# Two kinds in one slot: 84 half tiles in 42 slots in place of 45 whole tiles

## The reference

```python
x = x + gnn(layernorm(x), src/dst edges, edge_type)
t = layernorm(x)
hs     = gelu(t @ sw1[n].T + sb1[n])         # 2 shared experts, hidden 64 each
shared = sum_n hs[n] @ sw2[n].T + sb2.sum(0)
probs  = softmax(t @ gate_w.T + gate_b)      # 8 routed experts
cw     = probs where among the top 2 of a row, else 0
hr     = gelu(t @ rw1[e].T + rb1[e])         # hidden 64 each
routed = sum_e cw[:, e] * (hr[e] @ rw2[e].T + rb2[e])
x = x + shared + routed
```

## Time and profile before

| | us |
|---|---|
| median of 3 runs (lowest, highest) | 1600.99 (1600.15, 1612.06) |
| the profiled execution's own time | 1598.47 |
| its span | 1596.7 |
| PE busy | 1491.6 (93%) |
| DVE, ACT, POOL busy | 927.9, 705.7, 662.6 |
| five bare slots, 1459.68 to 1514.16 | 54.48 |
| four slots with group work, 1247.66 to 1299.35 | 51.69 |

### The profile page before, as it was taken

One profiled execution on the slowest core, in us unless ns is written; L12 is line 12 of the kernel. 1 busy time (PEld: TensorE's weight loads), 2 busy tenths in 40 slices (PEclk: granted clock), 3 DMA queues, 4 the chain that ended last, 5 costly groups with the idle time before them and its releaser, 6 DMA issues. The chain is left out here.

```text
span 1596.7 us, 27768 instructions
## 1 busy us (share of the span) xinstructions
PE 1491.6 (93%) x8680; PEld 1200.0 (75%) x8680; DVE 927.9 (58%) x2667; ACT 705.7 (44%) x1231; POOL 662.6 (41%) x989
## 2 busy tenths in 40 slices
PE   6999998989898999999999986599999999999997
PEld 4777666777786677777888864478888888888986
DVE  5555686867752333334766556566666767665453
ACT  3334334556652212122666535446565656453322
POOL 3762232457753000000467634546546464543222
PEclk9999999999999999999999998699999999999999
DMA  9999999597757999999667688879776776534220
GB/s 243 277 279 286 298 294 304 190 289 131 128 91 170 295 290 279 278 292 272 157 126 133 106 214 175 236 204 249 224 233 191 221 213 200 167 129 131 93 75 3
DMA packets 130212, 325.95 MB, mean 204 GB/s; under 512 B 17115, under 2 KB 17641, under 8 KB 129698
## 3 DMA queue, kind: packets, MB, share of 16 engines
q1 hardware_dynamic: 84626, 211.19, 44.8%
q0 software_dynamic: 45456, 113.12, 31.1%
HBM read 205.62 MB, written 121.74 MB: 205 GB/s over the span
## 5 line engine op out<-in xcount | busy, mean ns | idle before, releaser
L1207 ACT ACTIVATE th<-bank 128x512 fp32r<-128x512 f32 x158 | 94.2, 597 | 291.7 <-PE bank L1487 291.6
L1005 POOL DMA_INDIRECT gx<-y,dst_slot x42 | 46.2, 1101 | 266.1 <-ACT xn_e L1227 243.0
L1842 DVE SCALAR_TENSOR_TENSOR tl<-bank,th 128x512 fp32r<-128x512 f32 x79 | 54.4, 689 | 162.3 <-ACT th L1207 162.0
L1139 POOL DMA_INDIRECT out<-xt,out_row x90 | 93.2, 1035 | 128.4 <-DVE xt L2198 92.3
L1467 PE MATMUL bank<-root2h,th 128*128 128x512 f32 x316 | 133.1, 421 | 12.6 <-DVE tl L1842 7.8
L1467 PE MATMUL bank<-root1h,th 128*128 128x512 f32 x316 | 131.6, 416 | 7.9 <-DVE yout L1869 4.8
L1869 DVE TENSOR_TENSOR yout<-bank,bias_b 128x512 f32<-128x512 f32 x150 | 102.3, 682 | 45.4 <-DMA y<-yout 18.7
L1467 PE MATMUL bank<-root2l,th 128*128 128x512 f32 x316 | 126.0, 399 | 0.0
L1467 PE MATMUL bank<-root2h,tl 128*128 128x512 f32 x316 | 125.2, 396 | 0.0
L1467 PE MATMUL bank<-root1l,th 128*128 128x512 f32 x316 | 125.0, 396 | 0.0
L1467 PE MATMUL bank<-root1h,tl 128*128 128x512 f32 x316 | 124.1, 393 | 0.0
(11 more groups left out here) (355 smaller groups left out, 4378.8 us busy)
## 6 DMA issues: line engine op xcount, KB each, us to landing
basis_t<-in_gnn_basis SPq DMA_DIRECT2D x64, 896.0 KB
xt<-sorted_rows SPq DMA_DIRECT2D x45, 560.0 KB, 3.9
xin<-in_x SPq DMA_DIRECT2D x39, 512.0 KB, 8.8
xin<-y SPq DMA_DIRECT2D x39, 512.0 KB, 8.5
y<-yout SPq DMA_DIRECT2D x37, 512.0 KB, 9.2
z<-yout SPq DMA_DIRECT2D x34, 512.0 KB, 8.4
stage1q<-in_x SPq DMA_DIRECT2D x5, 1024.0 KB, 7.5
stage2q<-in_x SPq DMA_DIRECT2D x5, 1024.0 KB, 8.7
```

The lines of the kernel that those rows point to most:

```text
L1005: pool.indirect_dma_start(out=gx[:, e % 6, :], out_offset=None, in_=x if pr.phase == SB else y1, in_offset=bass.IndirectOffsetOnAxis(ap=ds ...
L1139: pool.indirect_dma_start(out=out, in_=xt[i % 4][:, j, 0:H], in_offset=None, out_offset=bass.IndirectOffsetOnAxis(ap=out_row[:, i % 4, j:j ...
L1207: act.activation(th_a[:, s, :], tpb[s][:], f).then_inc(s_hi, 1)
L1842: ins = dve.scalar_tensor_tensor(out=tl_a[:, s, :], in0=tpb[s][:], scalar=0.0, in1=th_a[:, s, :].bitcast(F32), op0=ALU.max, op1=ALU.subtract)
```

## The change

A tile keeps its 256 rows, but each half (128 rows) is chosen, loaded and multiplied with a kind of its own. The regions of the table are laid out for 128-row pieces, there are 84 half tiles in 42 slots (`NF` = 42), and what was read once per tile is read once per half: SP reads two row numbers and issues two loads of 128 rows, DVE picks twice, reads four chunk numbers and multiplies by the shares in four pieces, PE reads six numbers and takes the up- and down-weights of each half by registers of that half. POOL computes the rows of a tile that were done before for each half. Six zero stores of 128 rows stand in place of twelve.

```diff
-    KIND = FW + N
+    KIND = P + N
-    NF = (N + NKIND * (FW - 1)) // FW
+    NF = ((N + NKIND * (P - 1)) // P + 1) // 2
...
             for k in range(NKIND):
-                for j in range(2):
-                    first = HEAD + k * KIND + j * P
-                    sp.dma_start(sorted_rows[first:first + P, :], zeros[:]).then_inc(s_pads, 16)
+                first = HEAD + k * KIND
+                sp.dma_start(sorted_rows[first:first + P, :], zeros[:]).then_inc(s_pads, 16)
...
-                r = sp.value_load(pick_int[0:1, i, 0:1], min_val=0, max_val=XROWS - FW)
-                sp.dma_start(xt[i % 4][:], sorted_rows[bass.ds(r, FW), :].rearrange("(p j) w -> p j w", j=2))\
-                    .then_inc(s_xt[i % 4], 16)
+                for j in range(2):
+                    r = sp.value_load(pick_int[0:1, 2 * i + j, 0:1], min_val=0, max_val=XROWS - P)
+                    sp.dma_start(xt[i % 4][:, j, :], sorted_rows[bass.ds(r, P), :]).then_inc(s_xt[i % 4], 16)
...
                 for c, j in itertools.product(range(2), range(2)):
-                    if j == 0:
-                        pe.wait_ge(s_gs, 2 * i + c + 1)
+                    pe.wait_ge(s_gs, 4 * i + 2 * c + j + 1)
                     ins = pe.transpose(b[:, c * FW + j * P:c * FW + (j + 1) * P], gelr[:, j, c * P:(c + 1) * P], ident[:])
...
             def picked(i):
                 pe.wait_ge(s_pick, i + 1)
                 tops = (len(CHAIN) - 2, FC - 1, FC - 1)
-                return [pe.value_load(pick_int[0:1, i, c:c + 1], min_val=int(c > 1), max_val=tops[c - 1]) for c in (1, 2, 3)]
+                return [[pe.value_load(pick_int[0:1, 2 * i + j, c:c + 1], min_val=int(c > 1), max_val=tops[c - 1])
+                         for c in (1, 2, 3)] for j in range(2)]
...
-                slot, chunks = chosen[0], chosen[1:]
+                chunks = [row[1:] for row in chosen]
                 for j in range(2):
-                    ins = up_routed(i, j, slot)
+                    ins = up_routed(i, j, chosen[j][0])
...
-                down_routed(i, 0, chunks)
+                down_routed(i, 0, chunks[0])
                 if exists(i + 1):
                     turn_tile(i + 1, "x")
                     chosen = picked(i + 1)
-                down_routed(i, 1, chunks)
+                down_routed(i, 1, chunks[1])
...
+            def pick_tile(i):
+
+                q = group_of_pick(i)
+                dve.wait_ge(s_qpos, q + 1)
+                for j in range(2):
+                    pick_half(2 * i + j, q)
+                link(dve.tensor_copy(pick_int[0:1, 2 * i:2 * i + 2, :], pick[0:1, 2 * i:2 * i + 2, 0:4]))
                 dve.sem_inc(s_pick, 1)
...
-                chunks = [dve.value_load(pick_int[0:1, i, c:c + 1], min_val=1, max_val=FC - 1) for c in (2, 3)]
-                for c in range(2):
-                    weigh(i, c, chunks[c])
+                chunks = [[dve.value_load(pick_int[0:1, 2 * i + j, c:c + 1], min_val=1, max_val=FC - 1) for c in (2, 3)]
+                          for j in range(2)]
+                for c, j in itertools.product(range(2), range(2)):
+                    weigh(i, c, j, chunks[j][c])
```

More of the change, by code:

```diff
@@ L176, in gnn_moe_kernel @@
         e_scan = sb("e_scan", [ER, EC])
+        e_f_at = top[0]
         e_f = sb("e_f", [ER, 4, EC])
@@ L180, in gnn_moe_kernel @@
         e_iota = sb("e_iota", [ER, EC])
+        e_end = top[0]
         n_col = sb("n_col", [P, 4], I32)
@@ L198, in gnn_moe_kernel @@
         lim_base = sb("lim_base", [P, 2, NKIND])
-        row_index = sb("row_index", [P, 2])
+        row_index = sb("row_index", [P, 1])
         token_base = sb("token_base", [P, QT])
@@ L203, in gnn_moe_kernel @@
         again_row = sb("again_row", [P, QLAST])
-        hidden_part = sb("hidden_part", [P, 1])
+        hidden_part = sb("hidden_part", [P, 2])
         far_row = sb("far_row", [P, 2])
@@ L265, in gnn_moe_kernel @@
         lim = sb("lim", [P, 2, 2, NKIND])
-        pick = sb("pick", [P, NF, 6])
-        pick_int = sb("pick_int", [1, NF, 4], I32)
+        pick = sb("pick", [P, 2 * NF, 6])
         pick_key = sb("pick_key", [P, NKIND])
@@ L271, in gnn_moe_kernel @@
         assert top[0] <= gatew0_at + 4 * R * H
+        pick_int, pick_end = place("pick_int", [1, 2 * NF, 4], I32, at=e_f_at)
+        assert pick_end <= e_end
         b1r = place("b1r", [P, len(CHAIN), P], F32R, at=gatew0_at + 4 * R * H)[0]
@@ L860, in _ @@
             load_group(5)
-            sp.wait_ge(s_pads, 16 * 2 * NKIND)
+            sp.wait_ge(s_pads, 16 * NKIND)
             load_tile(0)
@@ L929, in iota @@
                               allow_small_or_imprecise_dtypes=True).then_inc(s_pool, 1)
-                iota(kinds[:, 4, :], [[KIND, NKIND]], HEAD + FW)
+                iota(kinds[:, 4, :], [[KIND, NKIND]], HEAD + P)
                 iota(lim_base[:, 0, :], [[KIND, NKIND]], HEAD)
                 iota(lim_base[:, 1, :], [[1, NKIND]], 0)
-                iota(row_index[:], [[1, 2]], 0, 2)
+                iota(row_index[:], [[0, 1]], 0, 1)
                 iota(token_base[:], [[1, QT]], 0, QT)
@@ L937, in kind_tables @@
                 iota(again_row[:], [[1, QLAST]], 0, QLAST)
-                pool.memset(kinds[:, 5, :], float(FW)).then_inc(s_pool, 1)
+                pool.memset(kinds[:, 5, :], float(P)).then_inc(s_pool, 1)
                 for k, (a, b, slot) in enumerate(KINDS):
@@ L1124, in rows_of_tile @@
                 pool.wait_ge(s_pick, i + 1)
-                pool.wait_ge(s_xt[i % 4], 16 * (i // 4 + 1))
-                pool.tensor_tensor(hidden_part[:], pick[:, i, 4:5], pick[:, i, 0:1], ALU.subtract).then_inc(s_rows, 1)
+                pool.wait_ge(s_xt[i % 4], 32 * (i // 4 + 1))
+                pool.tensor_tensor(hidden_part[:], pick[:, 2 * i:2 * i + 2, 4], pick[:, 2 * i:2 * i + 2, 0], ALU.subtract).then_inc(s_rows, 1)
                 pool.wait_ge(s_rows, 4 * i + 1)
-                pool.tensor_scalar(far_row[:], row_index[:], hidden_part[:, 0:1], FAR, ALU.is_lt,
+                pool.tensor_scalar(far_row[:], hidden_part[:], row_index[:, 0:1], FAR, ALU.is_gt,
                                    ALU.mult).then_inc(s_rows, 1)
@@ L1627, in turn_tile @@
                 if part == "a":
-                    pe.wait_ge(s_xt[i % 4], 16 * (i // 4 + 1))
+                    pe.wait_ge(s_xt[i % 4], 32 * (i // 4 + 1))
                 wait_turn_bank(pe, part, i)
@@ L2155, in positions, with pick_half @@
                     link(dve.tensor_tensor(posf[:, 0:n], posf[:, 0:n], again_row[:], ALU.add))
[L2156 to L2161, removed]
+                dve.tensor_scalar(pos[:, q % 4, 0:n], posf[:, 0:n], float(P), None, ALU.add).then_inc(s_qpos, 1)
+            def pick_half(n, q):
                 limit, far, last = lim[:, q % 2, 0, :], lim[:, q % 2, 1, :], kinds[:, 4, :]
@@ L2168, in pick_tile @@
                                               op0=ALU.is_equal, op1=ALU.mult))
-                link(dve.tensor_reduce(pick[:, i, :], pick_all[:], AX_X, ALU.add))
-                dve.tensor_copy(pick_int[0:1, i, :], pick[0:1, i, 0:4])
+                dve.tensor_reduce(pick[:, n, :], pick_all[:], AX_X, ALU.add)
                 link(dve.tensor_tensor(last, last, pick_all[:, 5, :], ALU.add))
+            def pick_tile(i):
[4 more added lines that the diff above has]
+                link(dve.tensor_copy(pick_int[0:1, 2 * i:2 * i + 2, :], pick[0:1, 2 * i:2 * i + 2, 0:4]))
                 dve.sem_inc(s_pick, 1)
@@ L2178, in f_lo, with weigh @@
                 dve.tensor_tensor(to[0], turn_bank(part, i)[:], to[1].bitcast(F32), ALU.subtract).then_inc(s_flo, 1)
-            def weigh(i, c, chunk):
+            def weigh(i, c, j, chunk):
                 dve.wait_ge(s_ger, i + 1)
-                part = gelr[:, :, c * P:(c + 1) * P].rearrange("p j (e f) -> p j e f", e=2)
-                share = xt[i % 4][:, :, bass.ds(2 * chunk + (WHOLE - 2), 2)].rearrange("p j (e a) -> p j e a", a=1)
-                dve.tensor_tensor(part, part, share.to_broadcast([P, 2, 2, P // 2]), ALU.mult).then_inc(s_gs, 1)
+                part = gelr[:, j:j + 1, c * P:(c + 1) * P].rearrange("p j (e f) -> p (j e) f", e=2)
+                share = xt[i % 4][:, j:j + 1, bass.ds(2 * chunk + (WHOLE - 2), 2)].rearrange("p j (e a) -> p (j e) a", a=1)
+                dve.tensor_tensor(part, part, share.to_broadcast([P, 2, P // 2]), ALU.mult).then_inc(s_gs, 1)
             def shared_lo(i):
```

## The result

The changed kernel takes 1659.45 us, the median of 4 runs (1654.27 to 1671.93), against 1602.89 of the kernel before: the ratio is 1.0354, 95% interval 1.0282 to 1.0425. It is slower, within the range of 1644 to 1708 and 22 us under the 1682 forecast. The profiled execution took 1659.33 us with a span of 1657.6, which is 60.9 over the span before.

The account below looks back on a forecast made before the run. The prediction took PE, busy 93% of the span, as the bound, with its sequencer's register loads already at the edge. 1598.5 - 32.7 + 88 + 4.2 + 2 + 22 = 1682 us, range 1644 to 1708.

Parts of the forecast that it names:

- Three slots less: Loop over slots: the three slots that go are bare ones of 10.9 us each, -32.7 us.
- Six loads on PE: End of each slot: PE stands 2.0 us in bare slots (+20), 2.35 more in group-work slots (+68), together +88 us.
- TensorE's clock: In the loop: the new stands take the granted clock down 14 times, about 1.6 us each, +22, between 0 and 62.
- The rival in which the clock holds: In the loop: all as forecast but without falls of the clock, 1660 us; chance 28%.
- The loop's start: Before slot 0 and in the first slots: uncovered PE loads and later first and third tiles, +4.2 us, between 2 and 7.
- DVE's four products: On DVE: four products on half the columns in place of two, 0.05 us a slot, +2 us in all.
- its loads and picks: On DVE: two more register loads and longer picks fit into its idle time, nothing; 55 us if the loads' cover failed.
- the first rival: End of each slot: PE's added loads stay hidden, only the gain is left, 1570 us; chance 8%.
- SP, POOL, zero stores: Loads three slots ahead on SP, POOL's small instructions, and zero-store transfers far ahead of the loop: nothing.

Follow-up runs that it names:

- a_multi_both: Changed kernel with one three-register load per half on PE and one two-register load per half on DVE, no bounds checks: 1567.46 us, 0.9795.
- b_multi_both: Kernel before, 45 slots, with PE's three numbers in one load and DVE's two in one load, no bounds checks: 1597.45 us, 1.0017.
- b_six: Kernel before, 45 slots, with PE reading each slot's three numbers twice, six register loads at the old place: 1705.15 us, 1.0693.
- a_three: Changed kernel, but PE reads half 0's three numbers only and multiplies both halves with that kind's matrices: 1585.94 us, 0.9938.
- a_filled: Changed kernel with nine more products of the shared experts' kind on PE between the x transposes and the six loads: 1672.68 us, 1.0471.
- a_split: Changed kernel with half 0's three loads on PE moved ahead of `turn_hidden`, half 1's left at the old place: 1601.06 us, 1.0047.
- a_three_dve: Changed kernel, PE reading half 0's three numbers only, with DVE's four register loads moved ahead of the output additions: 1627.72 us, 1.0178.
- b_dve_loads: Kernel before with only DVE reading its two chunk numbers twice, four register loads in a slot: 1603.77 us, 1.0042.
- b_dve: Kernel before with DVE's part alone: four register loads, four products on half the columns, work of two picks per slot: 1617.26 us, 1.0137.

## Why the prediction came out right, and which steps did not

*Three slots less, -32.7.* Right: the marks have 3 x 10.92 = 32.8, and the 35 us, give or take 7, between a_multi_both and b_multi_both agree.

*Six loads on PE, +88.* Right in mechanism and place; b_six has it alone. The size was right in bare slots (2.0 forecast, 1.96 measured) and too large in those with group work: 2.35 forecast, 1.87 measured, 54 us in place of 68. There I doubled a mean of 2.25 us for three loads, which holds slow ones. Six took 4.16 in the mean of 29 slots, in place of 4.6: the added three took 1.9, the price of a bare slot.

*TensorE's clock, +22.* 11 falls of 1.57 are 17, where I had 14 of 1.6. That the stands bring the falls is shown by three runs: b_six has the stands alone and 13 falls, a_three all but the stands and none, a_filled most of the stands filled and none. Not every stand does: by the idle times of their timelines a_three has waits of 0.4 to 1.5 us in every second slot with group work and not one fall, a_split 1.8 to 2.3 in 11 of them and 5 falls, a_three_dve 1.9 to 2.9 in 13 and 13 falls, the changed kernel 1.1 to 2.6 in nearly every slot and 11. The rival in which the clock holds (1660) landed on the time and was wrong on the cause; that it is 0.6 us from the result is chance, since the stands it reckoned with were too long by about what the clock took. The Trainium skill (TensorE: Matmul & The Clock Gate, section "HAM oscillation — how this bites in real kernels") ties the fall to idle gaps longer than any stand here; 11 falls with no stand over 2.6 us disagree.

*The loop's start, +4.2.* Not shown. The mark of slot 2 lies 3.0 us later, but among the versions of the kernel before it lies anywhere from 1063.8 (b_multi_both) to 1070.9 (b_dve_loads), and most of that is there at slot 0 already. From slot 0 to 2 the changed kernel takes 30.5 us, the one before 30.1.

*DVE's four products, +2; its loads and picks, nothing.* The changed kernel shows nothing for them, and that is luck: PE's stands gave DVE the time. The step is wrong as reasoned. I set the loads against DVE's idle time before the products, 2.4 us a slot, and the longer picks against DVE's idle time in the same slots, and it is the same idle time. I also priced a load at 0.65 us, from the median; the 1.64 of the same row was no rarity: in b_dve three of the four loads took 0.8 to 1.7 us in nearly every second slot with group work. With PE's loads out of the way the step costs 17 to 22 us (slots 2 to 31 of b_dve take 389.2 us, of a_three 393.6, against 371.7). So the first rival's 1570 for hidden loads could not have come about by hiding PE's loads alone.

*SP, POOL, zero stores, nothing.* Right as far as can be told: a_multi_both has them all, and its gain is that of the three slots.

The sum by parts: -32.8 + 54.1 + 19.6 + 17.3 + 3.0 - 0.4 = 60.8. Of the 22 us between forecast and result, 14 are the stands with group work, 5 the clock, 3 the start and DVE's products.

## What to carry to other kernels

A register load belongs to the sequencer's time, not to the engine's: price it with its check (0.64 us here, 0.36 without, 0.30 for the load), count the work that stands queued in front of it, and read several numbers by one load. Take its price from the place where it will run: the same load took 0.30 us in one slot and 1.6 in the next. When two additions are each called free because the engine is idle, ask whether it is the same idle time; test them together, not one by one. A stand that a change brings can hide another, so after the first cure look again at who waits.

## What the runs showed of the hardware that was not expected

In bare slots a load of one register took 0.30 us, of two 0.52, of three 0.77: some 0.23 for each register more. The Trainium skill (Runtime: NRT & Kernel Launch, section "Instruction fetch mechanics") gives about 0.2 us per register for the loads of registers that the runtime makes from HBM. The loads here read `pick_int` in SBUF, and their 0.23 lies close to that.

Register loads have slow stretches. Of DVE's loads in b_dve 40 of 124 in slots with group work took over 0.6 us, none of 56 in bare slots. Slot 13's four are shown above (up to 1.60 us); those of the slot ahead of it:

```profile
L2258 DVEq TENSOR_LOAD <-pick_int x4: 298/298/306, 1200.1 to 1201.9; - x4
```

Busy time in the two slots' stretches, columns as in the earlier trace rows, the fast one first:

```profile
1200.00:1202.50 2.50, 2.32 (x27) 2.18 (x26) 1.52 (x4) 2.47 (x4) 0.00 (x0) 1.00 0.97 369
1213.50:1217.50 4.00, 3.49 (x28) 2.31 (x26) 0.94 (x2) 1.75 (x3) 2.90 (x6) 1.00 1.09 197
```

The DMA engines are busy in both, but move 369 GB/s in the fast one, all from SP's queue, and 197 in the slow one, all from POOL's. There POOL issues indirect stores to the output, but what moves is a transfer that POOL had issued just before them, at 1210.66: it adds `z` to a later group's rows (line 1105), and landed 8.3 us later, at 1219.0. The stores issued at 1212.30 and 1213.70 landed behind it, at 1219.7 and 1220.3. The issues from 1211 to 1218, with KB each and median us from issue to landing:

```profile
stage1q<-z POOLq DMA_DIRECT2D x1, 1024.0 KB, 8.3
out<-xt,out_row POOLq DMA_INDIRECT x4, 5.5
```

Of b_dve's 180 loads 56 ran while such a transfer was between issue and landing, and 39 of these took over 0.6 us; of the other 124 one did. The loads of a_split on PE go the same way: 32 of 48 beside such a transfer, 2 of 204 elsewhere. There is one of these transfers for each group, which is every second slot, and none in the bare slots. That the slow loads come with this transfer is thus shown; what the two share was not tried and stays open.
